# Token halves four entries apart in every expert stage, with the second half's sum and statistics ahead of the first half's choice of experts

## What is computed

```python
x = x + tanh(g_xattn[L]) * attention_L(layernorm(x), ctx_1024)
x = x + tanh(g_ffn[L])   * experts_L(layernorm(x))

# experts, in the form common to the four layers
p = softmax(x @ Wr)                       # L0: 40 columns, L1: 16, L2: 31, L3: 8
w = top_k(p)                              # 6, 2, 3, 2 of them kept as weights
for e in experts:                         # all are computed, weighted by w
    h = silu(x @ Wg[e]) * (x @ Wu[e])     # L0, L1 (glu); L2: gelu, L3: relu of x @ W1[e] + b1[e]
    out += w[:, e] * (h @ Wd[e])          # L2, L3: + w[:, e] * b2[e]
```

## Time and profile before

| | |
|---|---|
| median of 3 runs | 655.82 us (655.57 to 659.88) |
| the profiled execution | 655.92 us |
| its span in the trace | 654.1 us |
| DMA packets | 33134, 59.06 MB |
| TensorE's clock, in tenths, lowest slice of 40 | 8 |

### The profile page before, as it was taken

How to read it: one execution, slowest core, us unless ns; L and a number is a source line. 1 busy time by engine, 2 the same in 40 slices (tenths; PEclk the granted TensorE clock), 3 DMA queues, 4 the chain that set the end, 5 groups by cost and what they waited for, 6 DMA issues and landing times.

```text
span 654.1 us, 11738 instructions
## 1 busy us (share of the span) xinstructions
PE 594.5 (91%) x3429; PEld 433.6 (66%) x3429; DVE 502.1 (77%) x1287; ACT 360.2 (55%) x639; POOL 222.0 (34%) x438
## 2 busy tenths in 40 slices
PE   8898699978999878997999799999998999987996
PEld 6684588746776555874666556888865777754784
DVE  7857779978777357997753579999968888655996
ACT  6326345525666514553566157888824666632885
POOL 4211255432000212532112126888831000201783
PEclk9989889998999979999999899999997999998999
DMA  8225886210000005811000217777410000000771
GB/s 289 66 97 152 181 196 176 76 50 1 4 28 3 27 1 122 195 35 33 4 6 18 57 50 251 237 241 234 153 33 2 3 28 3 4 2 10 263 243 42
DMA packets 33134, 59.06 MB, mean 90 GB/s; under 512 B 6530, under 2 KB 22562, under 8 KB 33084
## 3 DMA queue, kind: packets, MB, share of 16 engines
q1 hardware_dynamic: 32508, 57.43, 30.1%
q10 hardware_dynamic: 576, 1.02, 0.4%
HBM read 53.61 MB, written 4.29 MB: 89 GB/s over the span
## 4 chain that ended last, share of the span: by engine, by line
PE 69%; DVE 16%; ACT 5%; issue 5%; SPq 3%; DMA 2%; POOL 1%; DVEq 0%; ACTq 0%
PE PS L734 11%; PE PS L736 10%; PE PS L735 10%; PE PS L983 5%; PE PS L891 4%; PE PS L966 4%; PE PS L572 2%; PE PS L963 2%; PE PS L1000 2%; DVE hid_lo L1595 2%; ACT pT L1273 2%; PE PS L939 1%; DVE qst L1649 1%; DVE PS L1589 1%; PE PS L920 1%
## 5 line engine op out<-in xcount | busy, mean ns | idle before, releaser
L475 POOL TENSOR_TENSOR wpair<-ring,ones_col 128x128 fp32r<-128x128 f32 (+1 forms) x150 | 80.0, 533 | 149.0 <-PE PS L736 125.0
L1273 ACT ACTIVATE pT<-PS 128x512 f32<-128x512 f32 x160 | 92.6, 595 | 46.0 <-PE PS L966 37.6
L1595 DVE TENSOR_TENSOR hid_lo<-PS,hid_hi 128x512 fp32r<-128x512 f32 x150 | 102.4, 682 | 1.8 <-ACT hid_hi L1182 1.3
L1182 ACT ACTIVATE hid_hi<-PS 128x512 fp32r<-128x512 f32 x150 | 88.9, 593 | 19.0 <-DVE PS L1589 18.5
L477 POOL TENSOR_TENSOR wpair<-ring,wpair 128x128 fp32r<-128x128 f32 (+1 forms) x150 | 93.2, 621 | 11.8
L734 PE MATMUL PS<-xhi,wpair 128*128 128x512 f32 x204 | 85.0, 417 | 6.0 <-POOL wpair L477 4.9
L735 PE MATMUL PS<-xlo,wpair 128*128 128x512 f32 x204 | 82.5, 404 | 0.0
L736 PE MATMUL PS<-xhi,wpair 128*128 128x512 f32 x204 | 82.3, 404 | 0.0
L1176 ACT ACTIVATE pT<-PS,ring 128x512 f32<-128x512 f32 x96 | 65.9, 689 | 17.6 <-PE PS L736 16.3
L734 PE MATMUL PS<-hid_hi,wpair 128*128 128x512 f32 x150 | 62.1, 414 | 6.8 <-DVE hid_lo L1595 6.4
L966 PE MATMUL PS<-qst,kz 128*128 128x256 f32 x256 | 64.6, 338 | 3.0 <-ACT pT L1273 3.0
(11 more groups left out here) (239 smaller groups left out, 1118.0 us busy)
## 6 DMA issues: line engine op xcount, KB each, us to landing
qst<-gates SPq DMA_DIRECT2D x42, 512.0 KB, 4.8
qst<-gates SPq DMA_DIRECT2D x42, 256.0 KB, 4.3
ring<-in_mlp SPq DMA_DIRECT2D x48, 128.5 KB, 3.3
ring<-in_glu SPq DMA_DIRECT2D x27, 192.0 KB, 4.6
kz<-keys SPq DMA_DIRECT2D x36, 96.0 KB
keys<-qst SPq DMA_DIRECT2D x6, 512.0 KB, 3.6
qst<-kfull SPq DMA_DIRECT2D x96, 4.0 KB
wq<-in_wq SPq DMA_DIRECT2D x3, 256.0 KB, 3.6
```

Of the source, the lines that this page charges most:

```text
L475: pool.tensor_tensor(wpair[:, pair, 0, c], w, ones, ALU.mult).then_inc(M["wstep"], 1)
L1182: act.activation(hid_hi[:, kept, :], PS[:, gate_bank(glu, kept), :], ACT.Copy).then_inc(M["hi"], 1)
L1273: act.activation(pT[:, w % 8, :], PS[:, 2 + w % 2, :], ACT.Exp, scale=sc).then_inc(A["p"], 1)
L1595: dve.tensor_tensor(hid_lo[:, kept, :], PS[:, gate_bank(glu, kept), :], hid_hi[:, kept, :].bitcast(f32), ALU.subtract).then_inc(M["lo"], 1)
```

## The change

- **Order of units.** Units are taken in the order: half 0 of entries 0 to 3, then both halves of entries 4 to n-1, then half 1 of entries 0 to 3 (`unit_at`). Half 1 is thus four entries behind. The weights of entries 0 to 3 are loaded and split a second time, n+4 in all.
- **Choice by halves.** `route` becomes `score` and `choose`, for one half each. On DVE the second half's sum, moments and variance stand between the two of the first half; its application, low part, score and choice stand between units 0 and 4. ACT makes exponentials per half, with up to three changes of function (`first_use`).
- **Rows.** The weights are turned per half in fp32 and split in two parts (`high_rows`, `low_rows`) instead of three in bf16; PE spreads the rows of the first eight units; one DMA per half saves them. The rows of entries 6 to 9 are requested in one go.
- **Exit.** Half 0's sum is taken four units before the end and turned, added and normalised between the last units. The second half's is done within the next attention (v = 9 to 18, in L2 v = 1 to 7), and its query projections move back (`Q_AT`).
- **Out of L0.** SP's refills of entries 4 and 5 stand ahead of key saves; keys are stacked after entry 12; L2's keys are made in attention 1, masks prepared there; L0's input is added on POOL, L2's by PE through a unit matrix; mask products move into attention 3; the output bias becomes a PE product; the split of the query weights goes in four parts between weight splits. DVE's bias preparation has two parts instead of three.
- **Fillers** at the entries (L572: 8, and 13, 22 or 10) and exits (16 and 6) are gone.

```diff
+        def unit_at(L, u):
+            n = ROUTE[L]["ENT"]
+            if u < AHEAD:
+                s, hf = u, 0
+            elif u < 2 * n - AHEAD:
+                s, hf = (u + AHEAD) // 2, u % 2
+            else:
+                s, hf = u - n + AHEAD, 1
+            return u, s, hf, u % KEPT, s % 2
...
                 if L == 0:
                     flag_keys()
                     save_keys(1)
+                    sp.wait_ge(ac["vo"], 1)
+                    fill_ring(0, w, cols, range(2, RING))
+                if L == 2:
+                    stack_keys(3, range(KSLOTS))
+                for s in (RING, RING + 1):
+                    ring_part(s, s, s % RING)
+                if L == 0:
                     save_keys(3)
-                    stack_keys(1, range(KSLOTS))
-                    save_gates()
-                    save_keys(2)
-                    shift_windows()
+                save_gates(0)
+                for s in (RING + 2, RING + 3):
+                    ring_part(s, s, s % RING)
+                save_gates(1)
...
+                sp.wait_ge(rows_saved, 32 * (L + 1))
+                for s in range(FIRST_ROW, FIRST_ROW + RING):
+                    row_part(s, s, s % RING)
+                for s in (2 * RING, 2 * RING + 1):
+                    ring_part(s, s, s % RING)
...
+                hidden_part(0)
+                for s in range(2 * RING if L == 2 else n + AHEAD):
+                    if s + 1 < n + AHEAD:
+                        hidden_part(s + 1)
+                    else:
+                        if L < 3:
+                            layer_norm(2 * L + 2, (0,))
+                    result_part(s)
...
+                    for u in range(5, 2 * n + 1):
+                        if u + 2 < 2 * n:
+                            up(*U(u + 2))
+                        if u == 2 * n - 4:
+                            turn_back(L, 0)
+                        down(*U(u - 1))
+                        if u < 7:
+                            spread(*U(u + 1))
+                        if u == 2 * n - 1:
+                            layer_norm(2 * L + 2, (0,))
...
+                score(L, 0)
+                if L == 0:
+                    ln_apply(1, 1)
+                if L > 0:
+                    add_half(1, 1, L, at["fin"], earlier(L)["fin"] + 2)
+                    ln_moments(1)
+                    ln_variance(1)
+                choose(L, 0)
...
+                    if glu:
+                        gated(0, 0, True)
+                        hid_of(0)
+                        unit(1)
+                        ln_turned(2 * L + 1, (1,))
+                        unit(2)
+                        score(L, 1)
+                        unit(3)
+                        choose(L, 1)
+                        unit(4)
+                        low_rows(1)
...
+                if glu:
+                    add_half(0, back_bank(L, 0), None, y_turned, NHALF * L + 1)
+                    ln_moments(0)
+                    ln_variance(0)
+                    unit(2 * n - 2)
+                    ln_apply(2 * L + 2, 0)
+                    unit(2 * n - 1)
...
+                lo(2 * n - 1)
+                ln_turned(2 * L + 2, (0,))
...
-                layer_norm(2 * L, (0,))
-                if L == 3:
-                    pe.wait_ge(A["ue"], B)
-                keep_busy(5, 6)
                 for a in range(HGRP if L == 2 else HGRP - 1):
                     project_queries(0, a, 2 + a)
...
-        Q_AT = (12, 16, 20, 24)
+        Q_AT = (20, 22, 24, 26)
...
+                    if v in (9, 10, 11, 14, 18):
+                        second_half((9, 10, 11, 14, 18).index(v))
+                    if L == 1 and 34 <= v < 44 and v % 2 == 0:
+                        prepare_masks((v - 34) // 2)
```

More of the change, by code:

```diff
@@ L19 @@
 from contextlib import ExitStack
+from functools import partial
 import numpy as np
@@ L425, in attention @@
+                if L == 2:
+                    with sp.Fori(3, n // RING) as i:
+                        for k in range(RING):
+                            ring_part(RING * i + k, RING * i + k, k)
+                            row_part(RING * i + k, RING * i + k, k)
+                for s in range(n if L == 2 else 3 * RING, n + AHEAD):
+                    both_parts(s)
+                    if L == 0 and s < 3 * RING + KSLOTS:
+                        stack_keys(1, (s - 3 * RING,))
             def attention(L):
@@ L768, in down @@
-                def down(unit, entry, kept):
-                    slot, hf = kept // 2, kept % 2
-                    if hf == 0:
-                        pe.wait_ge(M["wdown"], entry + 1)
-                    pe.wait_ge(M["lo"], unit + 1)
-                    c = slice(2 * P, 3 * P) if glu else slice(P, 2 * P)
-                    product(PS[:, hf, :], slot % 2, c, hid_hi[:, kept, :], hid_lo[:, kept, :], False).then_inc(M["y"], 1)
-                for hf in range(NHALF):
-                    up(hf, 0, 0, hf, first=True)
@@ L813, in experts @@
-                with pe.Fori(1, groups(n)) as i:
-                    for k in range(RING):
-                        for hf in range(NHALF):
-                            u = 2 * RING * i + 2 * k + hf
-                            up(u + 2, RING * i + k + 1, (k + 1) % RING, hf)
-                            if hf not in LOADED[glu]:
-                                spread(u + 2, RING * i + k + 1, (2 * k + hf + 2) % KEPT)
-                            down(u - 1, RING * i + (k if hf else k - 1), (2 * k + hf - 1) % KEPT)
@@ new lines, in experts, with step @@
+                U = partial(unit_at, L)
+                def step(u):
+                    if u < 2 * n - 5:
+                        up(*U(u + 4))
+                    down(*U(u))
+                    if u == 2 * n - 5:
+                        turn_back(L, 0)
+                        up(*U(u + 4))
+                    if u == 2 * n - 2 and L < 3:
+                        layer_norm(2 * L + 2, (0,))
+                for u in range(2):
+                    up(*U(u))
+                if L == 0:
+                    pe.wait_ge(rt["shift"], 1)
+                    for c in (KV_LN, KV_LN + 1):
+                        key_value(c)
```

1122 lines of the change are left out of this document (653 added, 469 removed).

## The result

The changed kernel takes 710.11 us (706.38 to 714.37, 4 runs) against 656.26 of the kernel before; the ratio is 1.081 (1.074 to 1.088). It is slower by 54 us where 10 less were forecast.

A forecast was written before the change was run, and what follows sets the result against it. PE, busy 91% of the span, was taken to bound the kernel, leaving only the seams to win or lose. Terms summed to -9.5 us on a 654.1 us span, giving 644.6 and a forecast of 646; range 629 to 668.

The forecast's parts named there:

- The stall in L0: L0's gap near 75 us: moving refills ahead of key saves removes PE's wait and half-clock matmuls, -7.5 us (5 to 8).
- Entries: Start of each layer's experts: first half's choice comes earlier, second's partly paid by DVE; L1 -6, L2 -2, L3 -1, L0 +3.
- The clock: Exits and entries without fillers: PE stands idle in places and runs at half clock there, +2 us (0 to 7).
- The clock rival: Three exits and three entries without fillers each pay half clock: 15 us in place of 2, 659 us; chance 0.09.
- Exits: End of a layer's experts: projections follow the last down product sooner, less DVE work between units; L0 -3, L1 -1, L2 -5.
- Attention starts and loops: Attention starts, DVE-bound, take over the second half's add and LayerNorm work: A1 +2.5, A2 +3.5, A3 +1; loops 0.
- Burst: Entries of L2 and L3: four rows requested together ahead of entry 8's refill delay its weights, +2.5 us each (0 to 6).
- Single-half entries: Last four units: POOL has one unit of time per split instead of two; +3.5 us in L3's tail (+1 to +5).
- Small ones: L0 residual adds and masks leave DVE, -2.5; fewer bias parts, -1; two PSUM operands in L2 and L3 products, -1.
- Given back: Seam gains are lost behind the seams, in attention starts and exits: 656 us, no change; chance 0.20.
- late weights: L2 and L3: POOL's splits and entry 8's refill come late, +20.5 us, 667 us; chance 0.20.
- the clock in the entries under 0.8: Sign named beforehand: a granted clock under 0.8 in the entries would show the forecast wrong.

The follow-up runs named there:

- experiment 5: Kernel before with SP's refills of entries 4 and 5 ahead of the second key save and entry 6's ahead of the first rows; 649.11 us against 655.65.
- experiment 11: Changed kernel with experiment 9's mends plus matmuls of zeros at two more waits of each entry; 683.00 us against 680.90.
- experiment 1: Kernel before without its fillers at entries, exits and ahead of the first projections; 667.08 us against 656.78.
- experiment 4: Changed kernel with POOL's root for the first half's LayerNorm ahead of the last but one result split; 698.64 us against 710.11.
- experiment 12: On top of experiment 10, attentions 1 and 3: second half's LayerNorm two steps earlier, query projections at steps 17, 21, 25, 28; 674.40 us against 678.04.
- experiment 8: Changed kernel with the refill of entry 8 ahead of the burst of four rows in L2 and L3; 704.10 us, 6.0 us faster.
- experiment 10: On top of experiment 9, in the last four entries POOL splits the last two's hidden parts one step earlier; 678.04 us against 680.90.
- experiment 9: Changed kernel with POOL's root earlier, fillers at entries, query projections three steps apart and entry 8's refill ahead of the burst; 680.90 us against 710.11.
- a swap on DVE: Changed kernel with the first half's choice of experts ahead of the second half's output sum, moments and variance; 721.01 us, 10.9 us slower.
- experiment 2: Changed kernel with 9, 16 and 13 fillers ahead of turning the first half's rows in L1, L2 and L3; 703.33 us against 710.11.

## Why the prediction was wrong

**The stall in L0 (-7.5).** Right, and confirmed alone: -6.5 (experiment 5). In the changed kernel the stretch gave -2.3 where -5.5 was forecast with the start and the entry in it. The two runs with the stall mended alone have -3.8 and -5.2 in this stretch, so L0's entry and the start together cost 1.5 to 2.9 us where +2 was forecast: no failed step here.

**Entries.** This is the first step that failed. I took the gain from when the first half's choice could begin and let DVE pay for the second half's, as work to be added: L1 -6, L2 -2, L3 -1. Measured were -2.1, +9.2 and +11.4, the last two with the burst in them. What the first half was to gain, it gained: in L1 its first down product is 9.8 us earlier, more than the forecast. It is lost by the fifth. The step left out that PE is in order too: `turn_rows(L, 1)` stands ahead of the fourth down product, so that both choices lie in one chain, one behind the other, with four short units (5.5 us in L2) between them that can't cover it. From the first down product to the fifth L1, L2 and L3 lost 6.4, 16.4 and 11.6 us; with the clock whole in L2 and L3 it is still 9.8 and 8.9 there (experiment 11). The trace of before had the sizes: from 239.22 to the end of this row DVE needs 7.8 us from the logits to the parts in L1, for both halves, against 1.37 us a unit.

```profile
246.61 0.43 DVE L1545 TENSOR_TENSOR pT<-pT 128x256 bf16<-128x256 f32 x1
```

The readings place the loss; a run in which the second choice isn't in the chain was not made, so this cause is argued and not shown. ACT's changes of function were called hidden and left out of the sum. They are in the chain of the changed kernel, 2.6 us in L1 and 1.3 in L2.

**The clock (+2).** The sum put 2 us on it (0 to 7). The fillers alone are worth 10.3 us in the kernel before (experiment 1), and the changed kernel's mean clock is 0.918 against 0.967. The clock rival had the right kind, 15 us, and a chance of 0.09; it was wrong to hold it apart from the others, since the added waits bring it with them. By experiment 1 the term of the sum was too small by a factor of five.

**Exits (-3, -1, -5).** The second step that failed. The seam itself closed as forecast: from the last down product to the first query projection it is 1.2, 0.9 and 1.1 us, where it was 8.8, 8.8 and 11.8. The time went in ahead of it, from the tenth last down product to the last, which takes 27.2, 27.5 and 21.1 us in place of 18.4, 16.5 and 11.4. The row that I named, the root behind a weight split on POOL, got no cost of its own. The split ahead of it waits for a sum that PE has yet to make, and DVE and then PE wait for the root behind it: a line across three engines, 5 to 8 us in L0, 3.5 in L1, 3.0 in L2 (experiment 4). With it out of the way the exits and starts are -0.2, +2.6 and +0.8 us against before, where -0.5, +2.5 and -4 were forecast.

**Attention starts and loops (+2.5, +3.5, +1).** The starts were priced by DVE; the work went on into loops in which PE has 61 of 64 and 72 of 73 us, and I had put nothing there. They cost 7.0 and 8.7 us, of which 4.3 and 5.0 are waits for the one bank of the second half's projections, which experiment 12 removes, with 1.5 and 3.3 us of the loops; A2, where the steps are other ones, 1.2. This is the largest part that no mend removes.

**Burst (+2.5 each).** In L3 3.4 us (experiment 8), as expected in kind and size; in L2 PE waited for nothing there. The 4.8 and 3.3 us taken for it are medians over all such transfers of the kernel, not times of one alone.

**Single-half entries (+3.5 in L3).** +3.4 and +1.3 in the steady part. PE did wait for POOL there, as forecast, and the size came out right by luck: POOL needs 1.7 us an entry in the changed kernel and not 2.4, and most of the 3.4 us was the order of its queue (experiment 10). The sentence that POOL's mean comes down when DVE is less busy had the right outcome for another reason: DVE is nearly as busy as before. (The 88 us from which the forecast took 1.37 us a unit hold 375 matmuls, 62.5 units and not 64; the marks give 63.0 us for 46 units, the same 1.37.)

**Small ones (-2.5 in L0).** Taking the adds and the masks off DVE gave nothing: L0's steady part is +0.2. It took 28.6 us for 14 units before, 2.04 us a unit, which is nine matmuls of 0.23: PE was full there, and DVE wasn't what it waited for.

**The rivals.** "Given back" and "late weights" each held a part, and the range ended at 668 since they were priced one at a time. Half clock, two choices in a chain, the root's queue and the loops came together, 54 us. The mends of experiment 9 add up. Of the signs that were named beforehand, the clock in the entries under 0.8 came true (0.67 and 0.74 in L2 and L3); PE waiting for POOL or the ring in L2's units 8 to 14 did not.

**What is open.** 17 us stay over the kernel before in the best form of the change (674.4 against 657.5). How much of the entries' loss a shorter second choice would give back, why a swap on DVE lengthens the exits, and which of the loop's waits sets the others, isn't shown.

## What to carry to other kernels

Moving work into the gap of a pipeline is priced by the whole order of every engine that it crosses: for each added wait write down what stands behind it in that queue, and follow it until it comes back; a root of 1 us cost 3 to 8 us an exit because it stood behind a wait for the very engine that needed it next. A split into halves needs enough units between them to cover the second half's latency, not its busy time. And a change made of many parts is best timed part by part: its one simple part, three refills moved up in a queue, was worth 6.5 us, and the rest of it, by difference, lost 60.

## What the runs showed of the hardware

Fillers on a zero tile, 135 in all at three entries and three exits, are worth 10.3 us of 656.8 on this kernel; the mean granted clock is 0.924 without them and 0.967 with them. Once the clock had fallen after a wait of 3.8 us it stayed at 1.2 GHz for 15 us (394.98 to 410) although PE was busy for 14.9 of these 15 us; with fillers in that wait (experiment 2) the first 14 us of the same work ran at 2.4 GHz. With the same code and other timing ahead of it the mean clock over 14 us of L3's entry was 0.53 in one kernel and 0.88 in another.

POOL's split of 128x128 weights takes 0.40 and 0.46 us in L2's steady part of the changed kernel, where it took 0.55 and 0.66; DVE is busy for 93% of the one stretch and 95% of the other. DVE's product there has one input from PSUM in place of none, and itself takes 0.70 us in place of 0.75. A change of function on ACT shows as a load of 1.28 us, with the next instruction 0.02 us behind it.
